# A sparse graph attention layer on one core: the order of its last steps

## The reference

```python
h = jnp.maximum(_layernorm(x, axis=-1), 0.0)
support = (h @ weight).reshape(-1, H, D).transpose(1, 0, 2)
f1 = jnp.einsum('hnd,hd->hn', support, weight_u[..., 0])[:, None, :]
f2 = jnp.einsum('hnd,hd->hn', support, weight_v[..., 0])[:, :, None]
masked = leaky_relu(f1 + f2, 0.2) * adj
m = jnp.max(where(masked != 0, masked, -inf), axis=2, keepdims=True)
e = where(masked != 0, exp(masked - m), 0)
attn = e / e.sum(axis=2, keepdims=True)           # 0 where the sum is 0
out = einsum('hnm,hmd->hnd', attn, support).transpose(1, 0, 2).reshape(-1, H * D) + bias
return x + out + h @ proj_w.T + proj_b
```

## Time and profile before

| | us |
|---|---|
| runs | 859.76, 863.06, 864.25 (median 863.06) |
| the profiled execution | 860.12, span 858.4 |
| PE busy | 710.9 (83%) |
| VectorE busy | 643.1 (75%) |
| POOL busy | 529.0 (62%) |
| ScalarE busy | 129.3 (15%) |
| HBM traffic | 345.9 MB, 403 GB/s over the span |
| gathers: 384 | median 6.2 from issue to landing |
| adjacency quarters: 256 of 1 MB | median 13.3 from issue to landing |

### The profile page before, as it was taken

How to read it: one execution, slowest core, us unless ns; L and a number is a source line. 1 busy time by engine, 2 the same in 40 slices (tenths; PEclk the granted TensorE clock), 3 DMA queues, 4 the chain that set the end, 5 groups by cost and what they waited for, 6 DMA issues and landing times.

```text
span 858.4 us, 11157 instructions
## 1 busy us (share of the span) xinstructions
PE 710.9 (83%) x3011; PEld 434.2 (51%) x3011; DVE 643.1 (75%) x2740; ACT 129.3 (15%) x467; POOL 529.0 (62%) x598
## 2 busy tenths in 40 slices
PE   2989999999956878887888888788888878888865
PEld 0656666666513545454555445354544445454454
DVE  4556666657446988879869798977979787886887
ACT  0223333333210111000001011000011100000010
POOL 4344455454467776667766667676766766676570
PEclk9999999999966989888879898887989888988789
DMA  9999999999999999999999999999999999999971
GB/s 307 422 407 393 416 422 416 407 423 413 419 410 384 385 401 402 388 405 384 402 393 374 399 374 405 383 404 384 390 396 375 406 366 400 359 403 401 397 302 53
DMA packets 63855, 329.82 MB, mean 384 GB/s; under 512 B 12795, under 2 KB 15560, under 8 KB 31024
## 3 DMA queue, kind: packets, MB, share of 16 engines
q1 hardware_dynamic: 43056, 286.28, 83.8%
q0 software_dynamic: 18432, 34.30, 11.1%
q10 hardware_dynamic: 2304, 8.52, 2.4%
HBM read 328.99 MB, written 16.91 MB: 403 GB/s over the span
## 4 chain that ended last, share of the span: by engine, by line
PE 42%; DMA 25%; DVE 24%; issue 4%; POOL 3%; ACT 1%; POOLq 0%; ACTq 0%; SPq 0%
DMA adj_raw<-in_adj 21%; PE ps_words L400 11%; PE ps_agg L461 9%; PE ps_agg L381 7%; PE ps_two L381 6%; DVE att L933 5%; PE ps_two L400 5%; DVE cand L787 3%; DVE base L943 3%; POOL att L717 2%; DMA att<-support_table,idx 2%; PE ps_score L445 2%; DMA att<-in_x 1%; PE ps_words L392 1%; DMA support_table<-att 1%
## 5 line engine op out<-in xcount | busy, mean ns | idle before, releaser
L717 POOL DMA_INDIRECT att<-support_table,idx x384 | 417.4, 1087 | 188.7 <-issue 105.8
L400 PE MATMUL ps_words<-adj_raw,pack_w 128*128 128x512 fp8e4 x640 | 186.7, 428 | 25.4 <-DMA adj_raw<-in_adj 25.3
L461 PE MATMUL ps_agg<-att,ident 128*128 128x260 f32 x640 | 176.3, 428 | 8.5 <-DVE att L933 8.5
L461 PEld LDWEIGHTS ps_agg<-att,ident 128*128 128x128 f32 x640 | 135.1, 218 | 41.6 <-issue 18.6
L400 PE MATMUL ps_two<-adj_raw,pack_w 128*128 128x512 fp8e4 x384 | 118.9, 457 | 24.6 <-DMA adj_raw<-in_adj 24.5
L400 PEld LDWEIGHTS ps_words<-adj_raw,pack_w 128*128 128x128 bf16 x640 | 62.1, 106 | 125.3 <-DMA adj_raw<-in_adj 39.8
L787 DVE MAX8 cand<-ps_words 128x8 f32<-128x128 f32 x320 | 67.1, 281 | 66.3 <-PE ps_words L400 66.3
L933 DVE TENSOR_TENSOR att<-att 128x1536 f32<-128x1536 f32 x64 | 109.4, 1750 | 0.4 <-ACT att L625 0.4
L708 POOL COPY record<-att 128x8 f32<-128x8 f32 x64 | 13.4, 209 | 117.4 <-ACT att L569 117.4
L400 PEld LDWEIGHTS ps_two<-adj_raw,pack_w 128*128 128x128 bf16 x384 | 38.7, 113 | 91.5 <-DMA adj_raw<-in_adj 40.0
L381 PE MATMUL ps_agg<-w_all,hT 128*128 128x260 f32 x256 | 63.0, 389 | 4.1 <-ACT hT L565 4.1
(11 more groups left out here) (118 smaller groups left out, 821.2 us busy)
## 6 DMA issues: line engine op xcount, KB each, us to landing
adj_raw<-in_adj SPq DMA_DIRECT2D x256, 1024.0 KB, 13.3
support_table<-att ACTq DMA_DIRECT2D x16, 520.0 KB, 8.8
att<-in_x SPq DMA_DIRECT2D x16, 512.0 KB, 6.7
out<-base SPq DMA_DIRECT2D x15, 512.0 KB, 14.1
att<-support_table,idx POOLq DMA_INDIRECT x384, 6.2
out<-base SPq DMA_DIRECT2D x4, 128.0 KB, 1.9
w_all<-in_proj_wT SPq DMA_DIRECT2D x2, 128.0 KB, 6.0
w_all<-in_weight SPq DMA_DIRECT2D x2, 128.0 KB, 6.3
```

Of the source, the lines that this page charges most:

```text
L400: mm = nc.tensor.matmul(ps_words[buffer_of(t)][:, k * 512:(k + 1) * 512], pack_w[:, u * UT + s, :], adj_low[:, n % HELD, s, k * 512:(k + 1 ...
L461: mm = nc.tensor.matmul(ps_agg[:, b, 0:ROW], ident[:] if k < OWN else onehotT[:, g % RING, b], gathered[:, g % RING, b, k], start=(k == 0) ...
L717: pool.indirect_dma_start(gathered[:, g % RING, b, k, :], None, table, bass.IndirectOffsetOnAxis(idx[:, g % RING, b, k:k + 1], 0), bounds_ ...
```

## The change

It touches the work from step 29 on.

- In step 29, VectorE splits and lists tile 60 right behind its picks, and tile 61 behind its own, in two `list_own(30, b, 1)`, ahead of the step's remaining work for older groups.
- ScalarE clears group 30's ring place by tile: the first half ahead of `exponential(28)`, the second behind it.
- POOL waits for each tile's list and clearing apart from tile 60 on, and takes the own gathers of tile 60 ahead of the spill gathers of group 29, and likewise those of tile 62 ahead of the spill gathers of group 30.
- In step 30, PE does `aggregate(28, 0)` ahead of the packing of tile 63 and `aggregate(28, 1)` behind it; `edge_refs(29)` now stands ahead of tile 63's third quarter.
- VectorE weighs tile 58 ahead of the picks of tile 63 and tile 59 behind their listing, and puts `output(28, 1)` behind `one_hot(31)`; in the next step it puts the output of tile 59 between the two weighings of group 30.
- At the end, the four check instructions stand behind the last weighing and `output(30, 1)`, and the two check matmuls behind the last aggregation.

```diff
--- before.py
+++ after.py
@@ -486,17 +486,16 @@
                         pack_unit(t, u)
 
             offsets(LATE)
+            aggregate(LATE - 2, 0)
             pack_places(TILES - 1)
             for u in range(UNITS // 2):
                 pack_unit(TILES - 1, u)
-            aggregate(LATE - 2, 0)
             edge_records(LATE)
             row_scores(LATE - 1)
+            edge_refs(LATE - 1)
+            for u in range(UNITS // 2, UNITS):
+                pack_unit(TILES - 1, u)
             aggregate(LATE - 2, 1)
-            for u in range(UNITS // 2, UNITS - 1):
-                pack_unit(TILES - 1, u)
-            edge_refs(LATE - 1)
-            pack_unit(TILES - 1, UNITS - 1)
 
             offsets(LATE + 1)
             aggregate(LATE - 1, 0)
@@ -504,18 +503,17 @@
             row_scores(LATE)
             aggregate(LATE - 1, 1)
             edge_refs(LATE)
-
             aggregate(LATE, 0)
+
             row_scores(LATE + 1)
             edge_refs(LATE + 1)
             aggregate(LATE, 1)
-
             aggregate(LATE + 1, 0)
+            aggregate(LATE + 1, 1)
             pe.wait_ge(s_check, 1)
             nc.tensor.matmul(ps_list[0:1, 0:1], missed[:, 2:3], ones_f[:], start=True, stop=True)
             nc.tensor.matmul(ps_list[0:1, 64:64 + TILES], ones_b[:], spilled[:], start=True,
                              stop=True).then_inc(s_missed, 1)
-            aggregate(LATE + 1, 1)
 
             pe.wait_ge(s_flag, 1)
             with pe.If(pe.value_load(flag[0:1, 0:1], min_val=0, max_val=1) > 0):
@@ -637,9 +635,13 @@
                     act.wait_ge(s_based, TILES)
                     for q in range(RING):
                         clear(q)
+                if g + 1 == LATE:
+                    clear(LATE, 0, 1)
                 if g > 0:
                     exponential(g - 1)
-                if g + 1 >= RING:
+                if g + 1 == LATE:
+                    clear(LATE, 1, 1)
+                elif g + 1 >= RING:
                     clear(g + 1)
                 distances(g + 1)
 
@@ -718,10 +720,10 @@
                                         bass.IndirectOffsetOnAxis(idx[:, g % RING, b, k:k + 1], 0),
                                         bounds_check=N - 1, oob_is_err=False).then_inc(s_gather[g % RING], 16)
 
-            def gather_own(g):
-                pool.wait_ge(s_idx_own, g + 1)
-                pool.wait_ge(s_cleared, g + 1)
-                for b in range(groups[g][1]):
+            def gather_own(g, n, at=0, size=GS):
+                pool.wait_ge(s_idx_own, n)
+                pool.wait_ge(s_cleared, n)
+                for b in range(at, at + size):
                     for k in range(OWN):
                         gather(g, b, k)
 
@@ -730,15 +732,17 @@
                 for b in range(groups[g][1]):
                     gather(g, b, OWN)
 
-            for g in range(G - 1):
-                gather_own(g)
+            for g in range(LATE - 1):
+                gather_own(g, g + 1)
                 gather_spill(g)
-            for b in range(GS):
-                pool.wait_ge(s_idx_own, G + b)
-                pool.wait_ge(s_cleared, G + b)
-                for k in range(OWN):
-                    gather(G - 1, b, k)
-            gather_spill(G - 1)
+            gather_own(LATE - 1, LATE)
+            gather_own(LATE, LATE + 1, 0, 1)
+            gather_spill(LATE - 1)
+            gather_own(LATE, LATE + 2, 1, 1)
+            gather_own(LATE + 1, LATE + 3, 0, 1)
+            gather_spill(LATE)
+            gather_own(LATE + 1, LATE + 4, 1, 1)
+            gather_spill(LATE + 1)
 
 
         @block.vector
@@ -925,9 +929,9 @@
                 v.tensor_tensor(shifted[:, 0:size, OWN], score[:, 0:size, OWN], ps_ref[:, 0:size],
                                 ALU.subtract).then_inc(s_shifted, 1)
 
-            def weigh(g):
+            def weigh(g, *only):
                 dve.wait_ge(s_exp, g + 1)
-                for b in range(groups[g][1]):
+                for b in only or range(groups[g][1]):
                     rows = gathered[:, g % RING, b]
                     r = rows[:, :, 0:HF].rearrange("p k (h d) -> p k h d", h=H)
                     v.tensor_tensor(r, r, rows[:, :, HF:].unsqueeze(3).to_broadcast([P, BLOCKS, H, HD]),
@@ -947,6 +951,9 @@
             list_own(0)
             for g in range(LATE):
                 n = pick_words(picks[g][0], 0)
+                if g + 1 == LATE:
+                    picked = split_words(picks[g][0], 1, n)
+                    list_own(LATE, 0, 1)
                 if g == 0:
 
                     dve.wait_ge(s_based, TILES)
@@ -959,11 +966,15 @@
                 if g >= 2:
                     output(g - 2, 0)
                 for t in picks[g][1:]:
-                    n = pick_words(t, 1)
+                    n = pick_words(t, 0 if g + 1 == LATE else 1)
                 if g > 0:
                     shift(g - 1)
-                picked = split_words(picks[g][0], len(picks[g]), n)
-                list_own(g + 1)
+                if g + 1 == LATE:
+                    picked = split_words(picks[g][1], 1, n)
+                    list_own(LATE, 1, 1)
+                else:
+                    picked = split_words(picks[g][0], len(picks[g]), n)
+                    list_own(g + 1)
                 if g >= 2:
                     output(g - 2, 1)
                 if g > 0:
@@ -977,31 +988,33 @@
             row_maximum(LATE - 1)
             output(LATE - 2, 0)
             shift(LATE - 1)
-            output(LATE - 2, 1)
+            weigh(LATE - 1, 0)
             picked = split_words(TILES - 1, 1, pick_words(TILES - 1, 0))
             list_own(LATE + 1, 1, 1)
-            weigh(LATE - 1)
+            weigh(LATE - 1, 1)
 
             one_hot(LATE + 1)
+            output(LATE - 2, 1)
             scores(LATE)
             list_spill(LATE + 1)
             row_maximum(LATE)
             output(LATE - 1, 0)
             shift(LATE)
+            weigh(LATE, 0)
             output(LATE - 1, 1)
-            weigh(LATE)
+            weigh(LATE, 1)
 
             scores(LATE + 1)
             output(LATE, 0)
             row_maximum(LATE + 1)
+            shift(LATE + 1)
+            weigh(LATE + 1)
+            output(LATE, 1)
 
             v.tensor_reduce(missed[:, 0:1], record[:, :, SLOTS - 1], AX_X, ALU.max)
             after(step(v.tensor_reduce(missed[:, 1:2], seg_top[:], AX_X, ALU.max)))
             after(step(v.tensor_single_scalar(missed[:, 1:2], missed[:, 1:2], float(WORDS), ALU.is_ge)))
             v.tensor_tensor(missed[:, 2:3], missed[:, 1:2], missed[:, 0:1], ALU.add).then_inc(s_check, 1)
-            shift(LATE + 1)
-            weigh(LATE + 1)
-            output(LATE, 1)
             output(LATE + 1, 0)
             output(LATE + 1, 1)
 
```

## The result

The changed kernel took 856.78 us (median of 13 runs, 853.34 to 858.87), the kernel before on the same chip 861.85 (13 runs, 859.13 to 864.25): ratio 0.9947, 95% interval 0.9933 to 0.9960, a gain of 5.1 us (3.4 to 5.8). The forecast was 860.7, a gain of 2.4 against the median known then. The direction was right; the gain forecast was less than half of the measured one. The profiled execution took 857.76 (span 855.9), 2.4 less than the profiled one of before. That this equals the sum is chance: up to the start of tile 62's picks (803.60 against 806.32) this profile is 2.7 us shorter, where the sum had no gain, and from there to the end it is 0.2 longer.

The account below looks back on a forecast made before the run. From 806.32 VectorE's ordered list bounds the kernel, broken by waits for PE's edge records behind aggregations. Gains of 2.3 + 0.1 = 2.4 us off the 863.06 median gave 860.7; own range 859.4 to 862, measured-time range 856.8 to 864.6.

Parts of the forecast that it names:

- the sum: Whole change: 2.3 us from VectorE's shorter waits plus 0.1 from moving the checks, a gain of 2.4 us.
- everything goes well: Rival: stream not pushed, aggregations meet a higher clock; gain 4.3 us, 858.7; chance 0.20.
- Part 1: Step 29, tiles 60 and 61 listed apart: 2.4 us hidden in the 5.78 wait; at most 1.0 to be had.
- Part 2: Gathers' new order: stream pushed by 1.0 us (bounds 0 and 1.6), eating Part 1's gain.
- Part 3: Step 30, aggregation ahead of packing: takes 4.6 us (4.1 to 5.4); edge_rec wait 1.2 instead of 2.7.
- Part 4: Tile 63's picks start at 820.1, not 821.22, gain 1.1 us; quarters 2 and 3 take 2.1, exp wait 0.5.
- Part 5: Last two steps: edge_rec wait 0.45 instead of 1.69; scores(31) at 838.8 against 841.10, gain 2.3 us.
- Part 6: Checks behind the last weighing: VectorE's move gives nothing, moving the two check matmuls gives 0.1 us.
- fixed tail: After the last row reference: exp, weigh, three aggregations and outputs, some 11 us, unchanged but for 0.1.
- lower-clock rival: TensorE not granted full clock between 806 and 830: 5.5 us against the forecast path, 866.2; chance 0.15.
- three signs of being wrong: VectorE waiting for tile 62's packing beyond 807, tile 63's picks behind 821.2, or clock at 0.50 after 814.
- POOL: Gathers nearly late: issue beside weigh(30, 0) stretched about 0.9 us, last gather landing at 838.9, level with scores(31).

Follow-up runs that it names:

- pe30_undone: Changed kernel with PE's step 30 order as before (aggregation behind packing tile 63's first half), VectorE's new order kept; ratio to before 1.0000.
- step29_only_b: Kernel before plus only step 29's listing by tile, ring clearing by tile and the new gather order; ratio to before 1.0012.
- warm: Changed kernel plus unread matmuls in three of PE's idle stretches (6, 8 and 10); ratio to before 0.9955.
- before_third: Kernel before, unchanged, run again on another chip; ratio to before 0.9990.
- after_third: Changed kernel, unchanged, run again on another chip; ratio to before 0.9951.
- weigh29_whole: Changed kernel with both weighings of group 29 behind the last tile's listing, as before; ratio to before 0.9971.
- warm_spill: Kernel warm with two more fills of unread matmuls and group 30's spill gathers behind two own gathers of tile 62, not five; 854.72 us, ratio to before 0.9916.

## Why the prediction was right, and where it was off

The mechanism held in its main part: without PE's aggregation in its wait for the stream there is no gain (pe30_undone). The number held by luck. The measured 856.78 is at the very edge of the range for the measured time (856.8 to 864.6), which was wide because the runs scatter; the forecast's own range, 859.4 to 862 with a gain of 1 to 3.7, missed both the time and the gain of 5.1. Of the 3.9 us between 860.7 and 856.78, 1.2 are the base (863.06 was the median of three runs, 861.85 that of thirteen) and 2.7 the gain. The gain is even above the 4.3 of the rival "everything goes well", but not by its mechanism: the two aggregations that were to gain by a higher clock took what the forecast gave them (4.65 against 4.6 at 803.45, 4.21 against 4.1 at 823.10).

**Part 1** held where its cover held. The cover is a wait of PE for the stream: 5.78, 3.79 and, on the slower chip, none; there part 1 cost 2.5 us in the trace, as the prediction said it would.

**Part 2**: step29_only_b at 1.0012 agrees with no gain and with a small push; the push of 1.0 us was not isolated.

**Part 3** held: 4.65 us for aggregate(28, 0) with its last two matmuls (803.45 to 808.10) against 4.6; edge_rec waits 0.87 and 0.73 against 1.2. That there is no gain without this move is shown by pe30_undone.

**Part 4** missed one term: quarters 2 and 3 took 3.37 us against 2.1, since PE had paused 2.32 us ahead of edge_refs(29) and packed at the lower clock (0.50 at 814 to 816). In warm, where unread matmuls fill that pause, the clock stays at 1.00 and these quarters take 1.06 and 1.08 each. Tile 63's picks waited 0.61 for the packing. Exp waits were 0.40 (0.5).

**Part 5**: waits 0.85 against 0.45; scores(31) 0.5 to 0.8 late. Behind them edge_refs(31) loses another 0.5, with the wait for an aggregation (838.81) that no part of the sum had.

**Part 6** failed in "fixed tail". From edge_refs(31) to the end it is 15.0 and 15.1 us in the profiles of after and 13.7 in both of before on the chips of normal speed, as aggregate(30, 1) runs at the lower clock in after (4.06 and 4.08 for ten, 2.44 in both of before). Forecast 36.0 and 49.6, measured 37.0 to 37.3 and 52.1 to 52.3. This is no matter of which execution was taken: on those chips the ten matmuls take 2.44 in every profile with PE's and VectorE's old order from step 30 on (before, before_third, step29_only_b), and 4.06 to 4.68 in every one with the new order of VectorE and no fill at this place (after, after_third, pe30_undone, weigh29_whole, warm). So the lower clock there goes with the new order, for 1.6 us, and the sum put nothing for it. Why it does is open: PE pauses for 1.75 us just ahead in before_third and in after alike. The two check matmuls gave more than their 0.1: the last aggregation starts 2.63 us behind the one before it, not 2.90.

**The sum.** Against the first profile of before these losses, 2.5 to 2.7 us, take all of the 2.4. Against before_third it is a gain of 2.9. So the step that failed in the sum is the last one of all: that the profiled execution's tail stands for the kernel's, only shifted by the median. Its tail was 2.9 us shorter than that of before_third, while its picks of tile 62 began 2.1 later, so the whole (860.12 against 860.97) gave no sign of it.

The lower-clock rival was half true: the clock did fall at a place it named (tile 63's second half) and at later ones. But in before it falls as well: in before_third the aggregations at 825.98 and 838.95 take 4.67 and 3.99 us. That this costs before more than it costs after is argued from these rows, not shown. Of the prediction's three signs of being wrong one came, the clock at 0.50 after 814. But the sign was badly chosen, and the argument against the rival ("before, with the same breaks, it was 1.00 from 814") was a misreading: rows 2 end at 816, and the same profile has 0.50 from 824 to 831. A slip in the rival's price: 5.4 in place of 4.1 adds 1.3, not 1.5.

**POOL**: no wait for gathers in after; the last gather was issued at 832.28, in the same moment as weigh(30, 0), and took 1.00, not 0.9 more. That the gathers come next was right: VectorE waits for them in warm (1.03) and in warm_spill (0.69).

**Open**: of the 5.1 us (3.4 to 5.8) the traces account for 2.9 behind tile 62's picks, and 3.9 between pe30_undone (in its slowest run) and after. One mild and one longer profile of before on these chips don't say how often either comes, nothing ahead of tile 62's picks shows the rest, and what makes the clock fall behind one pause and not behind another stays unknown.

## What to carry to other kernels

Before a sum is built on a tail, look at the granted clock in it and take a second profile: the same program had 52.1 and 55.0 us there. Work moved into a wait is free only while the cause of that wait holds; name it (here the stream) and ask what happens when it is ahead. When a sequence of short pauses leaves PE at the lower clock, unread matmuls in the pauses can keep it up, but here they paid only in the kernels where the next wait behind them was shortened too.

## What the runs showed of the hardware

A gather's issue on POOL is stretched if it starts while a weighing (two SBUF inputs, 1.75 us) already runs on VectorE, and not if it starts first or with it. In after, 60 of the 384 issues start 0.3 to 1.3 us into a weighing; they take 1.36 to 2.30 us, the longer the earlier they start, so that each ends about 2.6 us behind the start of that weighing. In this stretch weighings start at 815.44, 822.85 and 832.26:

```profile
815.93 2.15 POOL L719 DMA_INDIRECT att<-support_table,idx  x1 [0.30 <-issue]
...
823.60 1.87 POOL L719 DMA_INDIRECT att<-support_table,idx  x1 [4.22 <-DVE idx L851]
...
832.28 1.00 POOL L719 DMA_INDIRECT att<-support_table,idx  x1 [0.30 <-issue]
```

The inference that the Trainium skill makes (SBUF — State Buffer, "Who interferes with whom"), that such an instruction doesn't hold up descriptor generation, does not agree with 2.15 and 1.87 us against 1.00; what it says there of the order of issue deciding who waits does agree: the issue that starts 0.49 or 0.75 us behind a weighing is long, and VectorE's weighings of one tile take 1.75 to 1.81 us with such an issue beside them or without.
